# First attention's projections as three products of high and low parts, their order within a batch, and the order of the first loads

## What is computed

```python
q = (layernorm(x) @ Wq + bq)   # 100 x 256 by 256 x 256, per batch
k = (ctx @ Wk + bk)            # 361 x 192 by 192 x 256
v = (ctx @ Wv + bv)
x = x + softmax(clip(q k^T * scale)) v @ Wo + bo      # 16 heads of 16
x = x + ffn0(layernorm(x))     # 8 experts, the best one of each token
x = x + attention1(layernorm(x), ctx)
x = x + ffn1(layernorm(x))     # 64 experts, eight of each token, and a shared one
```

## Time and profile before

| | us |
|---|---|
| median of 3 runs | 689.67 (688.25 to 689.8) |
| the profiled execution | 689.11 |
| its span | 687.5 |

### The profile page before, as it was taken

One profiled execution on the slowest core, in us unless ns is written; L12 is line 12 of the kernel. 1 busy time (PEld: TensorE's weight loads), 2 busy tenths in 40 slices (PEclk: granted clock), 3 DMA queues, 4 the chain that ended last, 5 costly groups with the idle time before them and its releaser, 6 DMA issues.

```text
span 687.5 us, 15189 instructions
## 1 busy us (share of the span) xinstructions
PE 624.1 (91%) x4734; PEld 497.4 (72%) x4735; DVE 380.9 (55%) x1190; ACT 400.0 (58%) x962; POOL 252.9 (37%) x349
## 2 busy tenths in 40 slices
PE   2999989999998999898999999999888799999992
PEld 1787656666676999876888666666656799999991
DVE  5222567777662111138989745454974666666661
ACT  1445698999854343244766787777252455555551
POOL 6002355557836000011010000000043688888880
PEclk9999999999977999999999999999998999999997
DMA  6115910003542895013110010000033776777774
GB/s 156 32 48 178 342 63 2 2 1 106 186 123 92 297 316 187 31 36 83 50 34 1 10 43 2 2 1 1 1 96 94 223 195 179 194 190 184 194 191 126
DMA packets 75179, 73.76 MB, mean 107 GB/s; under 512 B 10966, under 2 KB 68340, under 8 KB 75000
## 3 DMA queue, kind: packets, MB, share of 16 engines
q1 hardware_dynamic: 67472, 62.87, 29.9%
q0 software_dynamic: 4816, 8.07, 5.8%
q10 hardware_dynamic: 2840, 2.17, 1.0%
HBM read 57.78 MB, written 15.31 MB: 106 GB/s over the span
## 4 chain that ended last, share of the span: by engine, by line
PE 60%; DVE 12%; ACT 10%; issue 7%; DMA 4%; POOL 4%; SPq 2%; DVEq 0%; POOLq 0%; ACTq 0%
PE psum L1274 6%; PE psum L1285 6%; ACT probs L796 4%; PE psum L629 3%; PE psum L643 3%; PE psum L1776 3%; PE psum L1798 3%; PE psum L1785 3%; PE psum L722 2%; PE psum L712 2%; DMA x_rows<-xc_dram,slot_rows 2%; PE psum L1824 2%; PE psum L2378 2%; PE psum L2380 2%; PE psum L2379 2%
## 5 line engine op out<-in xcount | busy, mean ns | idle before, releaser
L796 ACT ACTIVATE probs<-probs,negmax 100x361 f32<-100x361 f32 x128 | 68.9, 587 | 10.5 <-POOL probs L862 10.4
L875 DVE TENSOR_SCALAR_CACHE_REDUCE probs<-psum 100x361 f32<-100x361 f32 x128 | 60.7, 530 | 16.6 <-PE psum L712 16.6
L722 PEld LDWEIGHTS psum<-ident,probs 100*128 100x128 f32 (+1 forms) x384 | 38.0, 151 | 25.2 <-issue 16.7
L722 PE MATMUL psum<-ident,probs 100*128 100x100 f32 (+1 forms) x384 | 45.9, 256 | 10.8 <-ACT probsT L804 4.0
L862 POOL TENSOR_SCALAR probs<-probs 100x722 f32<-100x722 f32 x64 | 50.4, 788 | 5.1
L2268 POOL TENSOR_TENSOR xT_low<-kT_all,xT_high 128x1600 fp32r<-128x1600 f32 x1 | 3.6, 3557 | 129.4 <-ACT xT_high L2239 129.4
L1315 ACT ACTIVATE kT_all<-psum,kT_all 128x128 f32<-128x128 f32 x88 | 25.0, 369 | 41.9 <-PE psum L1274 41.9
L2378 PE MATMUL psum<-xT_high,we_high 128*128 128x400 f32 x128 | 45.1, 353 | 2.9 <-DVE v_all L2632 2.9
L2380 PE MATMUL psum<-xT_high,we_low 128*128 128x400 f32 x128 | 44.9, 351 | 0.0
L2379 PE MATMUL psum<-xT_low,we_high 128*128 128x400 f32 x128 | 44.7, 349 | 0.0
L1274 PEld LDWEIGHTS psum<-kT_all,v_all 128*128 128x128 f32 x352 | 40.6, 192 | 4.8 <-issue 4.5
(11 more groups left out here) (449 smaller groups left out, 1698.1 us busy)
## 6 DMA issues: line engine op xcount, KB each, us to landing
v_all<-in_L_ffn_W_dram SPq DMA_DIRECT2D x16, 1024.0 KB, 5.7
xs_dram<-zeros SPq DMA_DIRECT2D x1, 7424.0 KB, 23.5
kT_all<-coefT_dram SPq DMA_DIRECT2D x18, 400.0 KB, 4.2
v_all<-in_L_ffn_Wg_dram SPq DMA_DIRECT2D x36, 128.0 KB, 2.5
v_all<-in_L_ffn_Wu_dram SPq DMA_DIRECT2D x36, 128.0 KB, 2.7
v_all<-in_L_ffn_Wd_dram SPq DMA_DIRECT2D x36, 128.0 KB, 3.0
ctx_nat<-in_ctx_dram SPq DMA_DIRECT2D x16, 192.0 KB, 2.5
rank_rows<-rank_dram SPq DMA_DIRECT2D x18, 100.0 KB, 3.4
```

The lines of the kernel that those rows point to most:

```text
L722: last = nc.tensor.transpose(pT_ps[0:rows[t], t, hh * NQ:(hh + 1) * NQ], probs[:, n % NPB, hh, t * P:t * P + rows[t]], ident[0:NQ, 0:NQ])
L796: last = nc.scalar.activation(row, row, ACT.Exp, bias=negmax[:, n % NPB, hh:hh + 1])
L875: last = nc.vector.tensor_scalar(probs[:, n % NPB, hh, 0:NKV], psum[0:NQ, n % 2 * 2 + hh, 0:NKV], -CLAMP, None, ALU.max, ALU.max, accum_ou ...
```

## The change

- Keys, values and queries of the first attention become three products each of fp32r tiles. The high part of a context is the copy that ScalarE made before, now into an fp32r tile `ctxT0_high`; its low part is a new subtraction on VectorE (`ctx_low`, 96 partitions by 722). The transposed x is split by VectorE (two operations instead of one copy). The weights are split once, high parts by ScalarE, low parts by GpSimd. The moving context of the keys has one column more, of zeros (`NKV + 1`, 362).
- The order of a batch on TensorE is keys, values, transposes of x, transposes of the next context, queries; it was keys, transposes of x, transposes of the context, values, queries. On VectorE the low part of the next context comes behind the copies of the values.
- The loops run over three pairs of batches, and the fourth pair is written out without the last, unused transposes and without SP's wait for them.
- First loads: SP issues the context of batch 0, x in two halves (each with a semaphore of its own), the context of batch 1, Wo and its bias. ScalarE issues Wk (with a semaphore of its own), Wv and its bias, bk, Wq and bq.
- ScalarE copies the first context before it works on the weights, the scaled biases and the root. A root of one column stands first. It also copies the rows of ones and writes the column of zeros.
- GpSimd writes `zeros` first of all; TensorE does six products of zeros at the very start and two behind the first transposes. The memsets of `v_all` come behind the splits of the weights.
- The rest renames semaphores and moves their counts.

The core of the diff:

```diff
     def sp_load0(sp):
-        sp.dma_start(x[:, 1:B + 1, :], a["x"].rearrange("b q d -> q b d")).then_inc(x_loaded, 16)
         sp_ctx(sp, 0, 0)
+        for half in range(2):
+            of = slice(half * B // 2, (half + 1) * B // 2)
+            sp.dma_start(x[:, 1 + of.start:1 + of.stop, :], a["x"][of].rearrange("b q d -> q b d")).then_inc(x_loaded[half], 16)
+        sp_ctx(sp, 1, 1)
...
+    def act_load_weights0(act):
+        act.dma_start(wk0[:, :, :], a["L0_xattn_Wk"].rearrange("(c p) n -> p c n", p=DCC)).then_inc(wk0_loaded, 16)
...
-        sp.wait_ge(ctxT_in_psum, B - 1)
-        sp.sem_inc(ctx_loaded[0], 32)
...
     def pool_consts(pool):
+        nc.gpsimd.memset(zeros[:, :], 0.0).then_inc(consts_ready, 1)
         nc.gpsimd.memset(ident[:, :], 0.0).then_inc(consts_ready, 1)
...
+        pool_split_weights0(pool)
         v_heads = v_all[:, 0:B, :, :].rearrange("p b t (h e) -> p (b t h) e", e=32)
         nc.gpsimd.memset(v_heads[:, :, 16:17], 1.0).then_inc(consts_ready, 1)
         nc.gpsimd.memset(v_heads[:, :, 17:32], 0.0).then_inc(consts_ready, 1)
...
+    def pool_split_weights0(pool):
+        pool.wait_ge(w_high, 1)
+        nc.gpsimd.tensor_tensor(wk0_low, wk0, wk0_high.bitcast(F32), ALU.subtract).then_inc(w_split, 1)
+        pool.wait_ge(w_high, 2)
+        for c in range(2):
+            q = slice(0, DCC + c)
+            nc.gpsimd.tensor_tensor(wv0_low[q, c, :], wv0[q, c, :], wv0_high[q, c, :].bitcast(F32), ALU.subtract
+                                    ).then_inc(w_split, 1)
+        pool.wait_ge(w_high, 3)
+        nc.gpsimd.tensor_tensor(wq0_low, wq0, wq0_high.bitcast(F32), ALU.subtract).then_inc(w_split, 1)
...
+        def ctx_low(n, p):
+            dve.wait_ge(ctxT_ready, n + 1)
+            nc.vector.tensor_tensor(ctxT0_low[p][:, :, 0:NKV], ctxT_ps, ctxT0_high[p][0:DCC, :, 0:NKV].bitcast(F32),
+                                    ALU.subtract
+                                    ).then_inc(ctxT_split, 1)
+
+        ctx_low(0, 0)
...
+        def pair(i, end):
+            for p in range(2):
+                b = 2 * i + p
+                nc.vector.tensor_scalar(xn[:, :], x[:, b + 1, :], mv[:, b, 0:1], rstd[:, bass.ds(b, 1)], ALU.subtract,
+                                        ALU.mult).then_inc(xn_ready, 1)
+                dve.wait_ge(xnT_in_psum, b + 1)
+                nc.vector.tensor_copy(xnT_high[:, :, :], xnT_ps).then_inc(xnT_ready, 1)
+                dve.wait_ge(xnT_ready, b + 1)
+                nc.vector.tensor_tensor(xnT_low[:, :, :], xnT_ps, xnT_high[:, :, :].bitcast(F32), ALU.subtract
+                                        ).then_inc(xnT_low_ready, 1)
+
+                dve.wait_ge(v_in_psum, b + 1)
...
+                if not (end and p == 1):
+                    ctx_low(b + 1, 1 - p)
...
     def pe_project0(pe):
+        pe.wait_ge(consts_ready, N_ZEROS)
+        products_of_zeros0(o_zeros, 6)
         pe.wait_ge(consts_ready, N_FIRST)
...
         transpose_ctx(0, 32)
-        pe.wait_ge(w0_loaded, 16 * N_W0)
-        with pe.Fori(0, B // 2) as i:
+        products_of_zeros0(o_zeros, 2)
+
+        def keys(b, p):
+            pe.wait_ge(ctxT_ready, b + 1)
+            pe.wait_ge(w_high, 1)
+            for m in range(2):
+                for c in range(2):
+                    nc.tensor.matmul(k_mm[:, m, :], wk0_high[:, c, m * P:(m + 1) * P], ctxT0_high[p][0:DCC, c, :],
+                                     start=(c == 0), stop=False)
+            pe.wait_ge(w_split, 1)
+            for m in range(2):
+                for c in range(2):
+                    nc.tensor.matmul(k_mm[:, m, :], wk0_low[:, c, m * P:(m + 1) * P], ctxT0_high[p][0:DCC, c, :],
+                                     start=False, stop=False)
+            pe.wait_ge(ctxT_split, b + 1)
+            for m in range(2):
+                for c in range(2):
+                    last = nc.tensor.matmul(k_mm[:, m, :], wk0_high[:, c, m * P:(m + 1) * P], ctxT0_low[p][:, c, :],
+                                            start=False, stop=(c == 1))
+            last.then_inc(k_in_psum, 1)
+
+        def values(b, p):
+            pe.wait_ge(w_high, 2)
+            pe.wait_ge(w_split, 3)
...
+        def pair(i, end):
             for p in range(2):
                 b = 2 * i + p
...
+                keys(b, p)
+                values(b, p)
 
                 pe.wait_ge(xn_ready, b + 1)
...
+                if not (end and p == 1):
+                    transpose_ctx(1 - p, 32 * (i + p) + 32)
+
+                pe.wait_ge(w_split, 4)
                 pe.wait_ge(xnT_ready, b + 1)
...
                 pe.wait_ge(k_stored, 2 * b + 2)
                 for m in range(2):
+                    cols = slice(m * P, (m + 1) * P)
                     for c in range(2):
...
+                        nc.tensor.matmul(q_ps[:, m, :], wq0_high[:, c, cols], xnT_high[:, c, :], start=(c == 0), stop=False)
+                        nc.tensor.matmul(q_ps[:, m, :], wq0_low[:, c, cols], xnT_high[:, c, :], start=False, stop=False)
+                    if m == 0:
+                        pe.wait_ge(xnT_low_ready, b + 1)
...
     def act_project0(act):
-        act_std(act, 0)
-        act.wait_ge(w0_loaded, 16 * N_W0)
...
+        act_load_weights0(act)
+        act.wait_ge(consts_ready, N_FIRST)
+        nc.scalar.activation(exp_turn[:, :], eps_col[0:NQ, :], ACT.Sqrt)
+        for p in range(2):
+            nc.scalar.activation(ctxT0_high[p][DCC:DCC + 1], ctxT0[p][DCC:DCC + 1], ACT.Copy)
+            for part in (ctxT0_high[p][0:DCC], ctxT0_low[p]):
+                nc.scalar.activation(part[:, :, NKV], zeros[0:DCC, 0:2], ACT.Copy)
...
         take_ctx(0, 0)
-        with act.Fori(0, B // 2) as i:
+        act.wait_ge(wk0_loaded, 16)
+        nc.scalar.activation(wk0_high, wk0, ACT.Copy).then_inc(w_high, 1)
+        act.wait_ge(w0_loaded, 16 * N_W0)
+        for c in range(2):
+            q = slice(0, DCC + c)
+            last = nc.scalar.activation(wv0_high[q, c, :], wv0[q, c, :], ACT.Copy)
+        last.then_inc(w_high, 1)
+        nc.scalar.activation(wq0_high, wq0, ACT.Copy).then_inc(w_high, 1)
...
+        act_std(act, 0)
```

More of the change, by code:

```diff
@@ L303, in build @@
     consts_ready = sem("consts_ready")
-    x_loaded = sem("x_loaded")
-    w0_loaded, wo0_loaded = sem("w0_loaded"), sem("wo0_loaded")
-    N_W0 = 6
+    x_loaded = [sem(f"x_loaded{half}") for half in range(2)]
+    wk0_loaded, w0_loaded, wo0_loaded = sem("wk0_loaded"), sem("w0_loaded"), sem("wo0_loaded")
+    N_W0 = 5
     dve_step = sem("dve_step")
@@ new lines, in values @@
+        def values(b, p):
+            pe.wait_ge(w_high, 2)
+            pe.wait_ge(w_split, 3)
+            for t in range(3):
+                cols = slice(t * P, t * P + rows[t])
+                for c in range(2):
+                    q = slice(0, DCC + c)
+                    nc.tensor.matmul(v_ps[0:rows[t], t, :], ctxT0_high[p][q, c, cols], wv0_high[q, c, :], start=(c == 0),
+                                     stop=False)
+                    nc.tensor.matmul(v_ps[0:rows[t], t, :], ctxT0_high[p][q, c, cols], wv0_low[q, c, :], start=False,
+                                     stop=False)
+                    last = nc.tensor.matmul(v_ps[0:rows[t], t, :], ctxT0_low[p][:, c, cols], wv0_high[0:DCC, c, :],
+                                            start=False, stop=(c == 1))
+            last.then_inc(v_in_psum, 1)
@@ L636, in pe_project0 @@
                 last.then_inc(xnT_in_psum, 1)
-                transpose_ctx(1 - p, 32 * (i + p) + 32)
+                if not (end and p == 1):
+                    transpose_ctx(1 - p, 32 * (i + p) + 32)
+                pe.wait_ge(w_split, 4)
                 pe.wait_ge(xnT_ready, b + 1)
-                for t in range(3):
-                    for c in range(2):
-                        last = nc.tensor.matmul(v_ps[0:rows[t], t, :], ctxT0[p][0:DCC + c, c, t * P:t * P + rows[t]],
-                                                wv0[0:DCC + c, c, :], start=(c == 0), stop=(c == 1))
@@ L652, in pe_project0 @@
+                    if m == 0:
+                        pe.wait_ge(xnT_low_ready, b + 1)
+                    for c in range(2):
+                        last = nc.tensor.matmul(q_ps[:, m, :], wq0_high[:, c, cols], xnT_low[:, c, :], start=False,
+                                                stop=(c == 1))
                 last.then_inc(q_in_psum, 1)
+        with pe.Fori(0, B // 2 - 1) as i:
+            pair(i, False)
+        pair(B // 2 - 1, True)
     def act_project0(act):
-        act_std(act, 0)
@@ L656, in act_project0 @@
-        act.wait_ge(w0_loaded, 16 * N_W0)
-        act.wait_ge(parity_ready, 1)
-        for r in range(2):
-            nc.scalar.activation(bq0m[:, r, :], bq0[:, :], ACT.Identity, scale=parity[:, r:r + 1]).then_inc(bq_scaled, 1)
-        act.wait_ge(bq_scaled, 2)
+        act_load_weights0(act)
[5 more added lines that the diff above has]
+                nc.scalar.activation(part[:, :, NKV], zeros[0:DCC, 0:2], ACT.Copy)
```

(12 more changed lines are left out.)

120 lines of the change are left out of this document (61 added, 59 removed).

## The result

The changed kernel took 699.0 us (median, 698.26 to 700.29) where the kernel before took 689.73 in the same comparison: 1.0124 times the time, interval 1.0095 to 1.0152. It is 9.3 us slower; the forecast was 12 us faster. The profiled execution took 698.26 us. Among the experiments further down one (more products of zeros) has four of ten executions more than 1.5% above its fastest; its ratio leaves these four out.

The account below looks back on a forecast made before the run. The first stage was taken as bound by first-data arrival and order, then TensorE's products: 16.3 + 7 x 6.26 - 0.16 = 59.96 us for 71.92, 12.0 less, hence 677.7 against the median; 8-in-10 range 673.5 to 683.

Parts of the forecast that it names:

- What bounds the kernel, the parts of the first batch up to the keys: Start of first stage: arrival and order of data bound it; context lands 6.5 us, key weights split by 9.1 and 10.5.
- The first batch: First attention's batch 0: earlier context and warming on zeros end it at 16.3 us instead of 24.14, bounds 14.5 and 21.
- the first rival: Batch 0: GpSimd's moved memset holds VectorE's normalisation of x, TensorE waits up to 5 us, 682.7 us in all; chance 0.08.
- the warming rival: First batch: TensorE, waiting for weights at 8 to 12 us, falls back to the lower pace; 680.7 us; chance 0.08.
- The period: Each batch of the first stage takes 6.26 us for 6.83, with both new waits on VectorE's splits hidden.
- The later stages are as before: Everything behind the first stage keeps its time, so the whole gains the stage's 12.0 us.
- The slower rival: First-stage loop: VectorE's operations each wait for GpSimd, TensorE stands 3.8 us a batch, 704 us in all; chance 0.04.

Follow-up runs that it names:

- more products of zeros: Changed kernel with the v_all memsets before GpSimd's splits and float32 queries, plus more zero products in the first batch: 685.84 us over ten executions, 0.9867 times before.
- the memsets first: Changed kernel with the two memsets of v_all moved ahead of GpSimd's splits of the weights: 693.82 us, 1.0041 times the kernel before.
- memsets first, 31 more on VectorE: Changed kernel with v_all's memsets ahead of the splits, plus 30 one-element memsets and a wait at the start of VectorE's stream: 683.57 us, 0.9883 times before.
- kernel with float32 queries: Changed kernel with v_all's memsets ahead of the splits and the first attention's queries as four float32 products, Wq unsplit: 680.7 us, 0.9855 times before.

## Why the prediction was wrong

**What bounds the kernel, the parts of the first batch up to the keys: right.** Copy at 8.11 (forecast 7.7), key weights' high part done at 9.4 (9.1), the low part at 10.7 (10.5). The context itself had landed by 5.5 us, not at 6.5; ScalarE's own list hid that, so the copy's time was right by ScalarE's term and not by the landing.

**The first batch: wrong, 27.1 for 16.3 us.** The step that failed, and cost most, is the argument against the first rival. It said that VectorE's rows take about 1 ns a column, so none looks like a form that wants a second way into memory. The pace of a row didn't tell: xn has that same pace (0.40 us) in the steady batches and takes 7.16 beside the series. And most of the rows that I compared with read PSUM, not SBUF as xn does. The evidence for the rival was the better one: a row of the same operation, SBUF to SBUF, 5.94 us for two columns beside that memset. It got 0.08. Its size was too small as well: up to 5 us, where the order of the memsets costs 7.9 (5.86 in batch 0, 2.09 in batch 1). xn takes 6.8 us more, because VectorE is held through a series of GpSimd operations and not through one; TensorE waits for 3.30 of them, and the rest of the cost comes with the clock. By the Trainium skill (SBUF — State Buffer, Who interferes with whom) a VectorE instruction in a two-port mode and a GpSimd instruction exclude each other, and `tensor_scalar` is among those that can enter it; the trace agrees (7.16 us for 0.40), and the prediction quoted that rule and went by its own reading of a pace.

The other 4.9 of its 10.8 us stay with the memsets first. Three further terms were too small: x landed at 11.9 and not 10.8 (with the memsets first that is hidden, as xn is ready before the values end); ScalarE's wait for the value weights lasted until the last load of its queue, bq, had landed (12.99), where I had them in time, so the values began at 15.3 and not 12.0 (14.7 with the memsets first, 2.7 of the 4.9); and between that and the keys the clock fell, which the warming rival had right in kind (0.08).

**Batch 1: not in the sum.** 8.66 for 6.26 us. The low clock lasts into it, until 31.6.

**The period: 6.55 for 6.26.** Keys 2.05 (1.99) and values 2.16 (2.16) are right, so the interpolation between 256 and 512 columns held. The query's instruction is right too: twelve in 1.38 us, 0.115 for 0.109. Missed was a gap of 0.16 us ahead of the first of them, in each batch, which the profile puts to issue. The kernel with float32 queries has it too (1.04 us for the 0.87 of the earlier trace rows), so it isn't the split; what it is stays open. The sum of the stage: 10.8 + 2.4 + 6 x 0.29 = 14.9 us over the forecast, which is the 12.0 that were to be gained and the 2.9 that were lost. So the rival alone doesn't explain the miss: with neither hold (memsets first, 31 more on VectorE) the kernel takes 683.57 us, still 5.9 over the forecast and at the upper end of the range.

**"The later stages are as before": wrong, 6.3 us beyond the stage's 2.9.** This term stood at nothing without a reason, and no rival had it; the last loop loses 7.2 us. The trace of before shows that VectorE's subtraction escapes the hold by some 0.1 us in each iteration (GpSimd 0.81 to 0.83 us behind it); a change that adds 26 instructions to VectorE's program uses that up. The slower rival named the right pair of engines, but in the first stage, where it cost nothing in the steady batches: xn and both copies keep 0.40, 0.68 and 0.41 us, for 0.40 and 0.69 in the earlier trace rows.

What causes the pause of 0.12 us is argued, not shown: it moves forward as the code ahead grows, from entry 51 to 25 for 26 instructions, to 28 in the kernel with float32 queries (22 more than before, which entry for instruction would be 29), and out of the places ahead of the long rows with 57 more. The Trainium skill (Advanced Engine Details and Errata, ISA Cache) gives an engine's instruction store lines of 256 instructions; a line's end inside the loop would do this. No run here shows the store itself. What the trace does show is that no code is loaded meanwhile: the changed kernel has no transfer on an instruction queue between 552 and 686 us.

## What to carry to other kernels

A GpSimd series and a VectorE operation with its tiles in SBUF are not independent. Before moving either, look for rows of the same form that take several times their own time somewhere, and believe these over any argument from the pace; keep series of memsets and splits on GpSimd away from the moment when VectorE's result is waited for. Where an operation passes such a hold by a tenth of a microsecond, a change anywhere ahead in that engine's code can decide a stage that it doesn't touch, so compare all stages and not just the edited one. And in this kernel splitting a float32 product in three paid only where the moving operand is wide: with 362 and 256 columns it gained 0.41 and 0.54 us a batch, with 100 it lost 0.5.

## What the runs showed of the hardware

- VectorE's `tensor_scalar` of 100 x 256 beside a GpSimd series: 7.16 us for 0.40; of 128 x 2: 5.94 for 0.17.
- VectorE's subtraction of two SBUF tiles (128 x 768), with a GpSimd subtraction starting 0.68 or 0.69 us behind it: 3.55 to 3.59 us in ten rows of three kernels; 0.95 in 23 rows at 0.69 to 0.74 us, in thirteen at 0.47 to 0.65, and in all at 0.81 and more; with GpSimd 0.15 us ahead 2.75, 0.50 to 0.66 us ahead 1.23 to 1.38.
- fp32r products, each of which stands as one matmul, at 2.4 GHz follow each other at 0.166 us with 362 columns, 0.12 with 256 and 0.115 with 100; at 1.2 GHz at 0.30, 0.21 and 0.21.
- In two of fourteen traces TensorE stood still for 3.46 and 3.26 us in the first layer's experts, each time with one 16 KB transfer of instructions inside the stop.
- Twenty-six instructions more on one engine, executed while it was idle, cost 7.4 us of 690; thirty-one more brought the changed kernel 8.2 back.
